# Keys' exponentials times normalised rows, kept turned rows, and edge steps held inside the mixer

## The reference, cut to what matters

```
# graph layer, 100000 edges
tmp = relu(concat([h[src], w]) @ W1.T + b1);  h_N = segment_sum(tmp, dst)
# mixer, 4 layers
h = layernorm(x) * g1 + b1
q = softmax(h @ Wq * scale, over a head's 32 columns)
k = softmax(h @ Wk * scale, over all rows)
context = k^T (h @ Wv)   per head;   x = x + (q @ context) @ Wo + bo
h = layernorm(x) * g2 + b2;  x = x + gelu(h @ W1 + b1) @ W2 + b2
# experts: the two largest of 16 gate logits per row choose and weigh two experts
```

## Time and profile before

| | us |
|---|---|
| median of 3 runs | 2359.34 (2351.77 to 2360.32) |
| the profiled execution | 2356.42 |
| its span | 2354.7 |
| PE busy | 1992.1 (85%) |
| DVE busy | 1524.8 (65%) |
| POOL busy | 1373.6 (58%) |
| ACT busy | 925.8 (39%) |

### The profile page before, as it was taken

The page is one execution under the profiler, slowest core; times in us unless marked ns, Lnnn a source line. Parts: engine busy times, 40 slices in busy tenths (PEclk is TensorE's granted clock), DMA queues, the critical chain, the costliest instruction groups (busy, mean ns, idle before and its releaser), DMA issues.

```text
span 2354.7 us, 33082 instructions
## 1 busy us (share of the span) xinstructions
PE 1992.1 (85%) x10654; PEld 1640.4 (70%) x10654; DVE 1524.8 (65%) x3442; ACT 925.8 (39%) x1947; POOL 1373.6 (58%) x1125
## 2 busy tenths in 40 slices
PE   2359899999888999988899998889999785799990
PEld 1337677777776778877677787767778574788880
DVE  4758867776787777678767777876766457411116
ACT  1224444443444444444444434454444231233330
POOL 4156566677556666756666675666667501566650
PEclk7769999999999999999999999999999885899995
DMA  8652222233322233333222233322223521799997
GB/s 212 183 148 72 69 71 71 73 78 101 87 72 70 72 74 75 85 104 76 67 73 73 71 84 105 89 72 73 70 72 84 118 77 44 236 305 303 302 280 169
DMA packets 269780, 268.49 MB, mean 114 GB/s; under 512 B 146075, under 2 KB 203486, under 8 KB 269630
## 3 DMA queue, kind: packets, MB, share of 16 engines
q0 software_dynamic: 127488, 134.76, 23.7%
q1 hardware_dynamic: 138030, 131.85, 19.1%
q10 hardware_dynamic: 4112, 0.03, 0.1%
HBM read 230.37 MB, written 35.05 MB: 113 GB/s over the span
## 4 chain that ended last, share of the span: by engine, by line
PE 58%; DVE 18%; DMA 10%; ACT 5%; issue 5%; POOL 2%; SPq 2%; DVEq 1%; POOLq 0%; ACTq 0%
PE bank L1205 21%; PE bank L1314 14%; PE bank L433 3%; DVE zl L455 3%; PE bank L434 3%; PE bank L441 3%; DMA xs<-zn_d,slot_tok 2%; PE bank L1215 2%; PE bank L1432 2%; DMA aT<-attr_d 2%; PE bank L1254 2%; PE bank L1440 2%; DVE z L481 2%; ACT zr L449 1%; DMA y_d<-yo,slot_row 1%
## 5 line engine op out<-in xcount | busy, mean ns | idle before, releaser
L843 POOL DMA_INDIRECT G<-P_d,src_T x896 | 1141.9, 1274 | 658.5 <-DVE z L481 388.6
L481 DVE TENSOR_TENSOR z<-bank,G 125x512 f32<-125x512 f32 x448 | 288.4, 685 | 174.4 <-PE bank L441 122.0
L1205 PE MATMUL bank<-W_s,hid 128*125 128x256 f32 x1600 | 366.6, 383 | 26.3 <-DVE qe L1616 26.3
L449 ACT ACTIVATE zr<-z 125x512 fp32r<-125x512 f32 x448 | 266.4, 629 | 304.8 <-DVE z L481 272.6
L455 DVE SCALAR_TENSOR_TENSOR zl<-z,zr 125x512 fp32r<-125x512 f32 x448 | 295.9, 702 | 130.4 <-ACT zr L449 125.9
L1314 PE MATMUL bank<-TT,W_s 128*128 128x250 f32 (+1 forms) x1280 | 352.9, 428 | 0.0
L1205 PEld LDWEIGHTS bank<-W_s,hid 128*125 128x125 f32 x1600 | 296.2, 190 | 73.5 <-issue 30.8
L1314 PEld LDWEIGHTS bank<-TT,W_s 128*128 128x128 f32 x1280 | 238.0, 191 | 93.9 <-issue 2.3
L433 PE MATMUL bank<-zr,onehot 125*125 125x256 f32 x896 | 268.2, 332 | 29.5 <-DVE zl L455 29.3
L1013 ACT ACTIVATE hid<-bank,b_s 128x375 f32<-128x375 f32 x320 | 166.6, 522 | 191.4 <-PE bank L1314 167.2
L434 PE MATMUL bank<-zl,onehot 125*125 125x256 f32 x896 | 227.0, 284 | 0.0
(11 more groups left out here) (313 smaller groups left out, 3019.6 us busy)
## 6 DMA issues: line engine op xcount, KB each, us to landing
W_s<-in_L_ffn_w SPq DMA_DIRECT2D x64, 512.0 KB
hid<-in_L_ffn_w SPq DMA_DIRECT2D x64, 512.0 KB
G<-P_d,src_T POOLq DMA_INDIRECT x896
W_s<-in_L_mix_W SPq DMA_DIRECT2D x8, 1024.0 KB, 10.5
aT<-attr_d SPq DMA_DIRECT2D x224, 31.2 KB
attr_d<-hn SPq DMA_DIRECT2D x12, 246.1 KB, 3.7
X<-in_x SPq DMA_DIRECT2D x5, 560.0 KB
P_d<-es SPq DMA_DIRECT2D x25, 112.0 KB
```

Of the source, the lines that this page charges most:

```text
L449: nc.scalar.activation(zr[:, s, k, :], z[:, k, :], ACT.Relu).then_inc(r_done, 1)
L481: nc.vector.tensor_tensor(z[:, k, :], edge_bank[k][0:ET, :], G[:, ST * s + 2 * k:ST * s + 2 * k + 2, :].rearrange("p j d -> p (j d)"), ALU ...
L843: pool.indirect_dma_start(G[:, j, :], None, P_d[:, :], bass.IndirectOffsetOnAxis(ap=src_T[:, at:at + 1], axis=0)).then_inc(g_in[j], 16)
L1205: ins = pe.matmul(to[0:T, (j - a) * D:(j - a) * D + D], w, m, start=n == 0, stop=n == len(pairs) - 1)
```

## The change

1. **Context out of normalised rows.** The product with `Wv` leaves the key stage. `es` is multiplied with the normalised rows themselves (`hn` and `hn2` by turns, 256 columns per half), `ctxS` is 128 x 2 x 256. The sums of exponentials come from ACT's accumulator (`accum_out` into `piece_sum`) and are kept by two short DVE instructions per piece in `key_sum`. In the middle stage the context is divided, turned (four transposes), given gain and shift by ACT (`ctxF`), multiplied by `Wv`, masked, and only then by `Wo`.
2. **Turned rows kept.** SP writes each group's `TT` to DRAM (`nT_d`, 641 KB) in the key stage and loads it back for the queries. The second normalising, turning and shifting are gone (200 PE transposes, 100 DVE and 80 ACT instructions). ACT waits for the store of a group before it overwrites `TT`; PE waits for the load ahead of `queries`. `weights_A` of the next layer is issued after the product with `Wv`. In the row stage all three units of queries stand after the fifth edge step, and ACT takes that group's fourth step ahead of the turned queries.
3. **Edge steps.** The second group of layers 0 and 2 has three steps, so all 224 are done inside the mixer. The round count is loaded into registers ahead of it, and PE waits for the last addition to `agg` itself.
4. **Routing.** `top_two` of two groups before stands ahead of `rows_sum`. ACT makes the first half of `inv_tile`, DVE the second in two pieces; POOL makes none.

```
-        ST_K = [2, 2, 3, 2, 2]
+        ST_K = [[2, 3 - l % 2, 3, 2, 2] for l in range(L)]
...
+            def keep_normalised_T(l, g):
+                if g == 0:
+                    sp.wait_ge(nT_in, l * NG * 16)
+                sp.wait_ge(ring_act, ring_h1(l, g) + LNU + 1)
+                sp.dma_start(nT_d[g], TT[:, :, :].rearrange("p k n -> p (k n)")).then_inc(nT_out, 16)
...
                             act.activation(eT[:, h, a * T:b * T], ...
-                                           bias=nb[:, pc, h:h + 1], scale=SCALE).then_inc(ring_act, 1)
+                                           bias=nb[:, pc, h:h + 1], scale=SCALE, accum_out=piece_sum[:, pc, h:h + 1]).then_inc(ring_act, 1)
...
-                    first_norm(u0 + 4, u0 + 4 - RING_A)
+                    if g + 1 < NG:
+                        act.wait_ge(nT_out, (l * NG + g + 1) * 16)
+                        first_norm(u0 + 4, u0 + 4 - RING_A)
...
-                        for i in ((0, 1), (2,))[pc]:
-                            rows_at(r0, i, lambda j: [(TT[:, k, tt_cols(j)], Wv_s[:, k, :]) for k in range(KD)])
...
-                                ins = pe.matmul(to[:, 129 * h:129 * h + 129], es[:, j, 128 * h:128 * h + 128], V5[:, j, h, :],
+                                ins = pe.matmul(to[:, D * h:D * h + D], es[:, j, 128 * h:128 * h + 128], NORM[g % 2][:, j, :],
...
-                    if g + 2 < NG:
-                        normalised_T(l * SETS + set_q1(g + 2), ring_q1(l, g + 2))
...
-            for e in range(EG_LAST, NEG):
-                both(e)
...
-            pe.wait_ge(edges_done, 1)
+            pe.wait_ge(acc_done, pe.snap(rounds * NPAIR + 1))
```

More of the change, by code:

```diff
@@ L343, in build @@
         LNU = 2 * KD
-        RING_GA = 4 + LNU + GT
+        RING_GA = [4 + (LNU if g + 1 < NG else 0) + GT for g in range(NG)]
         RP = ((0, 2), (2, 3), (3, 5))
@@ L600, in sp_tables, with round_count, more_rounds @@
                 nc.sync.wait_ge(a_out[i], r * (len(range(i, AC, AB)) * 48) + len(range(i, AC, AB)) * 48)
[L604 removed]
+        def round_count(eng):
             eng.wait_ge(rounds_done, 1)
[L606 removed]
+            return eng.value_load(rounds_i[0:1, 0:1], min_val=1, max_val=ROUNDS)
+        def more_rounds(eng, rounds, tables, first, middle, last):
             with eng.If(rounds > 1):
@@ L716, in _ @@
                     load_rows(X_B[0], x, 0, x_in[0])
-                attr_steps(step_k(l, NG) + 1, step_k(l + 1, 0))
+                at += 2
+                for g in range(NG - 2):
+                    attr_steps(at, step_p(l, g) + 5)
+                    at = step_p(l, g) + 5
+                    sp.wait_ge(ring_full, ring_p(l, g) + 2 * NF)
+                    load_normalised_T(g + 2)
+                attr_steps(at, step_k(l + 1, 0))
                 if l + 1 < L:
@@ L995, in _ @@
                 q_softmax(0)
-                copy_tile(uM, uM - RING_A, ctxT[:, :, :], 128)
-                first_norm(ring_q1(l, 1), ring_q1(l, 1) - RING_A)
                 step(eM)
+                act.wait_ge(ring_full, uM + 1)
+                for k in range(KD):
+                    ins = act.activation(ctxF[:, k, :], RING[(uM - RING_A) % 3][:, k * D:k * D + D], ACT.Identity,
+                                         bias=ln_col(l, 1, k), scale=ln_col(l, 0, k))
+                ins.then_inc(ring_act, 1)
+                step(eM + 1)
                 queries_T(0)
-                step(eM + 1)
                 second_std(0)
@@ L1772, in _ @@
                         keep_stats(g, l * NT + g * GT + NT, a_aggr, a_mv)
-            for e in range(EG_LAST, NEG):
-                both(e, e, last=e == NEG - 1)
             dve_acc(NPAIR - 1, block_of(NPAIR - 1))
```

240 lines of the change are left out of this document (126 added, 114 removed).

## The result

The changed kernel takes 2422.39 us (median of 4 runs, 2416.51 to 2424.46), the kernel before 2358.34 beside it: ratio 1.027, 95% interval 1.0248 to 1.0292. On another chip the ratio of the same pair was 1.0225 (1.0202 to 1.0249). It is slower, by more than the forecast: 2371 with a range to 2402. The profiled execution has a span of 2420.0 us against 2354.7, and a mean granted clock of 0.912 against 0.936.

The account below looks back on a forecast made before the run. PE and DVE were taken as nearly equal limits in the key stage, PE as the limit in the row stage. Terms 21 + 12 + 15 - 11 - 19 - 5 = +13 on 2356.4 gave 2369, 2371 with half the median's 3 us; range 2333 to 2402.

Parts of the forecast that it names:

- Key stage, full groups: Wider context product and additions delay `hn`; two-step groups +2.1 us, three-step groups +1.2, extra steps +1.8 each; together +21.
- K3 still waits for ACT: Key stage: K3 waits for ACT to read K0, so dropped `V5` copies on DVE give only 0.1 to 0.2 us.
- Rival (e): Clock falls to half at PE's key-stage holes, doubling the context product, +4.7 in 16 groups: 2446; chance 0.08.
- Rival (b): Full key groups keep 17.08 us, PE's slack or DVE's order absorbing the additions; middle at lower bound: 2343; chance 0.22.
- First groups: Key stage: the store of `TT` behind the weights delays the step, +4.0 in three layers, +0.3 in layer 0: +12.
- Middle stage: `M_s` stands behind an edge step on DVE and attention ends later, partly at low clock: +3.7 a layer, +15.
- Row stage: Ten transposes gone, but the hole waits for DVE: -1.0 twelve times, later copies 4 x 0.2; together -11.
- all 1.55: Row stage's lower bound, -19: the ten transposes' whole 1.55 us to the next PE work is gained.
- Mixer's end: The two steps after the mixer go, so PE reaches the sums earlier, -16.9, and -2 for turning: together -19.
- Routing: Last logits some 2.1 us earlier with `top_two` in DVE's wait, one-hots -2.6: together -5.
- Rival (d): Load of `TT` lands over nine us after issue, stopping PE at `queries`, 3 us in twelve groups: 2407; chance 0.13.
- Rival (c): Whole kernel: PE time is what counts, with -48, -34 and -24: 2253; chance 0.05.

Follow-up runs that it names:

- tail_only: The kernel before with parts 3 and 4 of the change alone (edge steps and routing): 2347.6 us, ratio 0.9945.
- pool_late: `kept_filled` with POOL's additions to `X` held back until the first turning behind the mixer: 2310.6 us, ratio 0.9767.
- kept_filled_routed: `kept_filled` with the old place of `top_two`, behind the experts' input: 2316.0 us.
- act_order: The changed kernel with ACT's copies of turned queries ahead of its fourth step again, queries still together behind the fifth: 2402.3 us, ratio 1.0170.
- row_order: The changed kernel with the row stage in the old order, on PE, DVE and ACT: 2405.1 us, ratio 1.0196.
- kept_filled: Changed kernel without part 1, old row order, kept rows in two buffers, first `aT` before first store, 4 idle products in the row stage's hole: 2318.3 us.
- narrow context: Changed kernel with context product and additions 129 columns a half, 127 left zero: 2388.7 us; with key-stage holes also filled by idle products: 2379.2 us.

## Why the prediction was wrong, step by step

**Key stage, full groups (+21; +39.5 measured).** Cut at the `z` of each group's last step, the difference is +3.3 up to the first group's, +16.1 in the second groups (12.0 forecast, with the extra steps), +10.3 in the third (4.8), +11.8 in the fourth (8.4), and -2.0 behind it (-4.4; the four terms given for it, -1.8, -1.7, +2.0 and +1.5, add to nothing and not to -1.1 a layer). The chain of a two-step group was right: 19.2 forecast, 19.07 at full clock. What failed is that it stopped there. The step "K3 still waits for ACT" was priced for DVE and not for what PE's holes do to its clock; that is 1.25 us in a two-step group. Rival (e) named this mechanism and got its place wrong: it doubled the context product, which runs at full clock in the trace, while the slow stretch lies on the turning and the edge steps, at a quarter of the price. The three-step group failed in its mechanism: the wait was said to vanish (+1.2). It moved, to 3.98 us in the turning, since ACT's reading of K2 stands behind the third step's work on DVE; the group grew by 2.7 us (22.3 against 19.6, layer 1) and is still 2.0 longer with the holes filled. The extra steps were undersized (1.8 against 3.4 each). Rival (b) falls: nothing absorbed the chain.

**First groups (+12; +9.1 in the last groups of three layers and +2.4 between the next layers' first two key steps).** Right, in mechanism and size: ACT waits for the store behind the weights, and with two buffers and `aT` ahead of the store these three last groups take 170.8 us and not 179.5 (170.3 before). 0.3 us were forecast for the first layer; 3.9 appeared ahead of the first key step. But `tail_only`, without any store, shows +3.6, and kernels with the store anything from +0.6 to +5.6, the changed kernel itself +1.8 in its other execution, so the 3.9 can't be told from the spread of executions.

**Middle stage (+15; +19.6).** The timeline was right to 0.4 us up to the end of attention. The remaining 1 us a layer lies behind it. Moving `M_s` back recovers 2.0 of the 3.3 that the step was charged with.

**Row stage (-11; +9.3).** This step failed outright, in two ways. "`out_rows` starts at 1239.5 and not at 1240.55" took the third unit of queries as hidden. It is not: its 2 us of PE stand behind the wait for DVE, where in the old order units two and three ran beside DVE's step. And the gain was sized too low at the same time: at full clock the old order with kept rows takes 939.5, against 963.8 less half of 10, 958.7, before: 19 us, the bound "all 1.55" for the ten transposes. The change had this gain and gave 18 us back by the order and another 10 by the clock (15 us, less the 5 that before loses too).

**Mixer's end (-19; -16.3 from the last row group's first step to the sums).** Two parts: from the turning of `es` to the sums -19.2, better than the -16.9 forecast. But POOL's additions to `X`, which follow the last gather, now fall into the last row group and hold a one-hot of DVE for 4.76 us; 3.2 us come back there (`pool_late`: 40.4 to 37.2), and the table has them in the last groups. The prediction did not ask what else was queued behind the moved gathers on POOL.

**Routing (-5; +0.2 and -2.3 from the first sums to the end in two executions).** The one-hots gave their share: from the last logits to the product with `inv_row` that gives the slots' weights 41.7 us became 39.4 (forecast -2.6), no one-hot over 3.5 us. The other half, earlier logits, isn't there: from first sums to last logits 112.8 us before, 112.8 and 115.8 in two executions of the changed kernel. With the old place of `top_two` it is 116.6 (`kept_filled_routed`), with the new place 111.4 and 115.5 in two executions of one kernel. That spread is larger than the effect; it stays open whether there is one. One thing that works against it is in the traces: the first group's `X` is done 20.0 us after the first sums before, and 23.0 and 22.7 in the changed kernel, since POOL's additions fall beside it. What of that reaches the last logits, no run shows.

**Rival (d)** falls: PE never waits for DMA at `queries`; a load lands 5.0 us after its issue (median; 6.7 at most), and nine were left. **Rival (c)** falls for the whole, but holds for the row stage, where the ten transposes' PE time came back in full and each us at half clock cost half a us.

## What to carry to other kernels

Price a removed product by what PE does in its place: where PE was the second limit and becomes idle in pieces (here of one to four microseconds), the granted clock can fall, and every later PE instruction on the chain pays; look for half-clock windows behind each new hole, and try filling it with products that nothing reads, sized to the hole. When several units are put together behind one wait, only those ahead of the wait are hidden. A step that is moved takes along what is queued behind it on every engine, POOL's elementwise work included.

## What the runs showed of the hardware

- **A hole's length alone does not tell whether the clock falls.** In `act_order` holes of 3.38 and 3.36 us stand in two neighbouring groups; behind the first the granted clock was at half (8 passes in 3.68 us), behind the second at 1.00. Of the twelve such holes of a kernel, one in each group with queries to come, 9 were followed by a fall in the changed kernel and 2 in `act_order` (3.35 to 3.47 us each), 10 in `row_order` and 3 in the kernel before (2.1 to 2.5 us each). Behind the filled holes it did not fall in any of the filled kernels; the 11 us at half clock in the row stages of `kept_filled` lie elsewhere in them. The Trainium skill, TensorE: Matmul & The Clock Gate, Part 1, says that the gate follows how busy the array has been of late; the filled runs agree. The pairs of equal holes show that something besides the hole's length decides; what it is wasn't tested.
- **What half clock costs depends on who is the limit.** In the row stage 34 us of it cost 16.8. In the key stage taking away 88 us of it (113 to 25, narrow context) gave 14.7, a sixth; much of that chain runs over DVE and ACT.
- **POOL's elementwise work holds DVE.** A one-hot of 0.67 us took 4.76 beside POOL's additions, `X` 4.42 and 7.01 instead of 2.07, and before the change `zl` 7.47 instead of 1.29. Not every instruction is held: the `z` at 1916.87, which adds a PSUM bank to `G`, took its 1.29 us beside the same addition. The Trainium skill, SBUF — State Buffer, "Who interferes with whom", says that the two share a pair of ports by an exclusive lock; this trace agrees, and so do the one-hots of the routing, 3.49 us each once POOL's half was gone (3.40 and 6.07 in the earlier trace rows).
